# Down product of a quantised FFN: 128 stationary columns per token column in place of 121

## What is computed

```python
# layer 0: depthwise 25x25 convolution with a sparse mask (9x9 taps at a step of 3)
x = conv(x) * x + bias + x
# layer 1, on tokens t = (64, 3025, 96)
t = t + attn(layernorm(t))     # 96 -> 192, FFT over tokens, gate, inverse FFT, 192 -> 96
t = t + ffn(layernorm(t))
# ffn: every product takes operands rounded to fp8 (5 exponent, 2 mantissa bits), sums rounded to fp16
h = relu(qlinear(t, W1, b1))   # 96 -> 384
y = qlinear(h, W2, b2)         # 384 -> 96: the "down product"
```

## Time and profile before

| | |
|---|---|
| median of the runs shown | 5087.42 us |
| the profiled execution, first to last instruction (its time in the profile) | 5082.0 us |
| instructions | 121784 |
| TensorE matmuls busy | 4747.4 us, 93% |
| TensorE weight loads busy | 4227.9 us, 83% |
| VectorE busy | 3785.3 us, 74% |
| ScalarE busy | 3808.6 us, 75% |
| GpSimd busy | 2488.9 us, 49% |
| mean granted clock of TensorE | 0.964 |

### The profile page before, as it was taken

One profiled execution on the slowest core, in us unless ns is written; L12 is line 12 of the kernel. 1 busy time (PEld: TensorE's weight loads), 2 busy tenths in 40 slices (PEclk: granted clock), 3 DMA queues, 4 the chain that ended last, 5 costly groups with the idle time before them and its releaser, 6 DMA issues.

```text
span 5082.0 us, 121784 instructions
## 1 busy us (share of the span) xinstructions
PE 4747.4 (93%) x40842; PEld 4227.9 (83%) x40842; DVE 3785.3 (74%) x10870; ACT 3808.6 (75%) x7819; POOL 2488.9 (49%) x2603
## 2 busy tenths in 40 slices
PE   8999994699999999999999999999999999999974
PEld 7888884488888888888888888888888888888853
DVE  3444443247888888888888888888888888888884
ACT  3444442378888888888888888888888888888853
POOL 2335432144555555555555555555555555555542
PEclk9999997599999999999999999999999999999985
DMA  6777775256666666666666666666666666666541
GB/s 204 246 226 242 239 234 153 81 161 179 174 180 175 172 176 177 178 176 177 177 174 176 178 176 179 177 179 175 179 173 174 178 176 179 176 177 175 156 115 30
DMA packets 781423, 893.15 MB, mean 176 GB/s; under 512 B 236243, under 2 KB 689292, under 8 KB 768652
## 3 DMA queue, kind: packets, MB, share of 16 engines
q1 hardware_dynamic: 780556, 885.27, 63.5%
q10 hardware_dynamic: 264, 0.10, 0.0%
HBM read 500.64 MB, written 384.61 MB: 174 GB/s over the span
## 4 chain that ended last, share of the span: by engine, by line
PE 68%; DVE 8%; ACT 3%; issue 3%; DMA 0%; POOL 0%; DVEq 0%; POOLq 0%
PE ps L1021 12%; PE ps L1046 10%; PE ps L1033 10%; PE ps L1062 6%; PE ps L1061 6%; PE ps L1073 6%; PE ps L1085 5%; PE ps L1111 4%; PE ps L1122 4%; PE ps L1098 3%; PE ps L1133 1%; ACT ps L791 1%; DVE gv L946 1%; ACT spec L786 1%; DVE mean L896 1%
## 5 line engine op out<-in xcount | busy, mean ns | idle before, releaser
L721 POOL TENSOR_SCALAR gv<-gv 96x400 f32<-96x400 f32 (+1 forms) x512 | 599.6, 1171 | 1675.8 <-DVE xn L961 1587.6
L838 ACT ACTIVATE y<-ps 128x1089 f16<-128x1089 f32 (+1 forms) x512 | 572.9, 1119 | 328.7 <-PE ps L1111 328.7
L340 PE MATMUL cps<-toep,xin 114*128 114x190 f32 (+2 forms) x3456 | 775.9, 339 | 44.2 <-issue 25.5
L1046 PE MATMUL ps<-hid,fa 121*128 121x384 f32 (+1 forms) x2048 | 734.1, 441 | 82.9 <-DVE t L985 70.6
L1021 PE MATMUL ps<-fb,acol 100*96 100x100 f32 x7936 | 786.5, 252 | 15.0 <-DVE spec L953 14.5
L1021 PEld LDWEIGHTS ps<-fb,acol 100*96 100x96 f32 x7936 | 724.9, 164 | 25.3 <-issue 25.0
L286 ACT ACTIVATE xo<-cps 128x180 f32<-128x180 f32 (+3 forms) x576 | 367.4, 638 | 451.0 <-PE cps L343 451.0
L317 DVE SCALAR_TENSOR_TENSOR xo<-cps,xo 128x180 f32<-128x180 f32 (+3 forms) x576 | 362.7, 630 | 459.2 <-ACT xo L286 458.7
L1033 PE MATMUL ps<-w1t,xnt 97*121 97x192 f32 x3200 | 702.9, 330 | 0.7 <-ACT xnt L829 0.7
L1061 PE MATMUL ps<-w2t,spec 97*100 97x96 f32 x3968 | 673.2, 252 | 4.7 <-ACT y L838 4.7
L1062 PE MATMUL ps<-w2t,spec 96*100 96x96 f32 x3968 | 675.8, 252 | 0.0
(11 more groups left out here) (105 smaller groups left out, 10581.5 us busy)
## 6 DMA issues: line engine op xcount, KB each, us to landing
a_d<-arow SPq DMA_DIRECT2D x448, 288.0 KB, 3.9
acol<-a_d SPq DMA_DIRECT2D x192, 600.0 KB
xin<-in_items SPq DMA_DIRECT2D x96, 1008.0 KB
g_d<-mixed SPq DMA_DIRECT2D x256, 300.0 KB
tok<-x_d SPq DMA_DIRECT2D x64, 1134.4 KB
out<-o_sb SPq DMA_DIRECT2D x448, 136.1 KB
x_d<-xo SPq DMA_DIRECT2D x48, 990.0 KB, 11.9
grow<-g_d SPq DMA_DIRECT2D x128, 312.0 KB, 11.2
```

Of the source, the lines that this page charges most:

```text
L340: last = nc.tensor.matmul(ps[2 * (m % DEEP)][:, (r0 - o0) * GC:(r1 - o0) * GC], xb, toep[e % 2][0:GP, c, at * GC:(at + r1 - r0) * GC], sta ...
L721: nc.gpsimd.tensor_scalar(v, v, 0.0, None, ALU.max).then_inc(v_cut, 1)
L838: nc.scalar.activation(y16[n % 2][:, :, 0:w], ps[:, MIXP:MIXP + FM, 0:w], ACT.Copy).then_inc(y16_ready, 1)
L1046: nc.tensor.matmul(ps[0:M, ROW, 0:(s1 - s0) * H], fa[:, :], hid[part][:, 0:s1 - s0, :].rearrange("p j h -> p (j h)"), start=True, stop=Tru ...
```

## The change

The down product takes 128 columns of `hq` from j * 121 on: the 121 tokens of token column j and the 7 entries that follow. Its output covers 128 partitions of PSUM in place of 121; the last 7 aren't read. `hq` gets 8 more entries per row (492 in place of 484), so that the last piece stays inside of it, and is cleared once at the start.

```diff
-        hq = [sb(f"hq{s}", [128, FM, TOK], F8) for s in range(2)]
+        hq = [sb(f"hq{s}", [128, FM, TOK + 8], F8) for s in range(2)]
...
                 for v in y16:
+                    nc.vector.memset(v[:, :, :], 0.0)
+                for v in hq:
                     nc.vector.memset(v[:, :, :], 0.0)
...
                 for j in range(w):
                     for m in range(FM):
-                        last = nc.tensor.matmul(ps[0:U, DOWNP, C * j:C * (j + 1)],
-                                                hq[n % 2][:, m, j * U:(j + 1) * U], w2q[:, m, :],
+                        last = nc.tensor.matmul(ps[:, DOWNP, C * j:C * (j + 1)],
+                                                hq[n % 2][:, m, j * U:j * U + 128], w2q[:, m, :],
                                                 start=(m == 0), stop=(m == FM - 1))
```

## The result

The changed kernel takes 5047.06 us in the median of 4 runs (5035.8 to 5048.58), the kernel before 5087.9 (5086.44 to 5089.26): ratio 0.9919, 95% interval 0.9904 to 0.9935. It is 41 us faster.

What follows compares the result with a forecast made beforehand. TensorE was taken as the bound, with loads pacing its down matmuls. 45.1 + 0.8 + 6.4 - 0.7 = 51.6 us took the profiled 5082.0 to 5030.4; 5.4 carried over gave 5035.8, rounded up to 5037 (range 5028 to 5062).

Steps and rivals of the forecast that it cites:

- The load: Down product: fp8 loads of the full 128 columns are of a faster kind, near 100 ns instead of 137.
- Rival A: Down loads: no fast kind for hq, 128 columns are just 7 more; 17.6 us slower, 5105 us; chance 0.07.
- B: Down loads: only pieces starting at a multiple of 4 bytes load fast; 5.4 us gained, 5082 us; chance 0.06.
- Term 1, spacing: Down matmuls at full clock: 43 ns each; nine take 0.387 us, 0.103 less, and twelve 0.516, 0.144 less.
- rival C: Down matmuls: loads fast, but no load and matmul pair starts sooner than 52 ns; 15.8 us gained, 5072 us; chance 0.05.
- Term 1, images: Long stretch: 0.762 us saved per image, 45.1 us over 59.2 images, and 0.8 us more up to 4917.
- 66 are on it: Of 75 down matmuls per image, 66 lie on the chain; the 9 beside the detour through VectorE's statistics are off it.
- Piece follows piece on TensorE, except once: Chain of one image: it leaves TensorE only at 3011.10, through ScalarE and VectorE's layernorm statistics, and returns at 3019.16.
- Rival D: Long stretch: another engine takes over in part of the slots; with half keeping their length 28.7 us gained, 5059; chance 0.03.
- part 4: Longer hq rows, four-column cast in three runs: counted at nothing; 0.3 us once per image, 1 us at most in the drain.
- Term 2, drain: From 4917 us: nine down matmuls take 0.72 us, saving 0.25 per slot, 6.4 us in all, all on the chain.
- Term 3, setup: Before the second stage: VectorE clears two hq buffers, 0.34 us each, 0.7 us together, hidden by nothing.

Runs made afterwards that it cites:

- e3_127: Changed kernel with 127 stationary columns in the down product in place of 128: 5090.4 us, ratio 1.0012 to the kernel before.
- e8_ib_128: Changed kernel with 128 stationary columns in place of 100 in the fp32 inverse transform too: 5097.2 us in one run.
- e1_flat: Changed kernel with hq's rows kept at 484 and only the whole buffer 8 entries longer: median 5035.5 us, ratio 0.9898 to the kernel before.
- e11_y_rows: Changed kernel with the rows of y, the cast's source, 8 entries longer too: 5036.1 us in one run.
- e2_pad: Kernel before with only hq's longer rows and its memset, down product still at 121 columns: median 5081.8 us, ratio 1.0004 to the kernel before.
- e12_pool_pad: Changed kernel, rows of 492, with the first part of the layernorm statistics moved from VectorE to GpSimd: 4943.5 us in one run.
- e7_turn2_128: Changed kernel with 128 stationary fp8 columns in place of 96 in turn2 too: 5048.3 us in one run.

## Why the prediction was right, and where it was off

**The load** (its unknown). Right: 98 ns measured, "near 100" forecast. e3_127 shows that the number of columns is what does it, and e8_ib_128 that fp32 doesn't get it; no run here has a type between the two. Rival A is out for 128 columns and is nearly what 127 do. B is out by the 4800 records. This is what the Trainium skill says on the page "TensorE: Matmul & The Clock Gate", section "Weight-path perf modes — Fast Weight Load (FWL) and DoubleRow": 128 weights, not FP32. The runs agree, at 127 against 128 columns and at fp8 against fp32. The size that the prediction quoted from this section of the Trainium skill, a load shorter by 4x in theory and about 2x measured, they don't confirm: the records shrank from 137 to 98 ns, 1.4 times, and as the moving side now sets the pace, the spacing can't tell how short the load itself is.

**Term 1, spacing.** 43 ns forecast, 42 to 43 measured: the line from 121 and 484 moving columns down to 96 holds, and rival C is out.

**Term 1, images.** Forecast 0.762 us per image, measured 0.61. Two steps failed.
First, "66 are on it": 57 are. The nine beside the detour were rightly left out, but the nine of the next slot are off the chain too, since TensorE waits there again for the residual sum. The slot stayed at 7.65 us, before 7.64. The trace of the kernel before had this wait already (0.41 us at 3026.68 where 0.35 is normal, and rows part 1 0.15 us behind the residual sum in every image); I had read "Piece follows piece on TensorE, except once". That is 0.10 to 0.11 us. The other five groups of nine gave 0.11 each and the twelve 0.15, a little more than counted, so that e1_flat comes to 0.71. Rival D named this mechanism, with a chance of 0.03; it holds in one slot of eight beyond the detour's, not in half. My argument against it, ScalarE's 0.59 us of slack in one slot, looked at the wrong engine: VectorE, busy for 3088 of 3600 us, has slack on average and none around its statistics. ScalarE's wait in that slot didn't fall to the 0.49 us of the forecast either; it is still 0.59 on average.

Second, part 4, "counted at nothing": the longer rows of hq. I bounded the cast's growth by 0.3 us and it was 0.75, and I took its slot as one "where hq isn't urgent", which is true for hq and false for VectorE's queue. e1_flat and e11_y_rows show that a shorter cast brings back 0.10 and 0.07 us per image, e2_pad that the long one costs nothing while slots are longer, e12_pool_pad that it costs nothing without the burst.

The way from the cast to the detour can be read in the traces: VectorE's operations end late where a two-input operation (TENSOR_TENSOR) of GpSimd runs beside them. The bias operations of 364 elements that meet none take 304 to 306 ns on average, 315 at most, in the kernel before, the changed one and e1_flat (2000 to 4500 us). All that take more than 330 ns, 199 of 850 before and 327 of 861 in the changed kernel (246 in e1_flat), meet one, and 246 of those 327 end 0.10 us after it. So the long cast shifts the bias operations behind it onto GpSimd's work, above all those of the next slot (306 ns on average before, 523 now, 319 in e1_flat). It is the same with L898: in 41 of 41 images of the kernel before and in 40 of 41 of the changed one it ends 0.10 us after GpSimd's multiplication L747 (L749). It starts 0.09 us ahead of that operation before and 0.19 us ahead of it in the changed kernel, so its greater length is GpSimd's operation coming later. By which operations the delay gets from the slots behind the cast to this one stays open, and no run took GpSimd's operations away.

**Term 2, drain.** A slot at the lower clock gained 0.26 us, as forecast. But from eviction 464 to the end only 1.7 us were gained, where the terms give about 8. The step that failed is again part 4, "1 us at most" for the casts there. Six casts of four columns fall into that stretch, and nothing hides the later ones: the slot behind each of the last three is 7.27, 7.27 and 7.13 us, and 6.52, 6.52 and 6.38 in e1_flat, 0.75 us apart. With rows of 484 the whole stretch is 299.8 us, 5.4 below the changed kernel and 7.1 below before. The rest, some 1 to 2 us, can't be told from scatter: e7_turn2_128, which differs from the changed kernel in turn2 alone, needs 2.1 us more for the stretch.

**Term 3, setup.** 0.73 us for the memsets, right. The first up eviction comes 2.2 us later, but in the fourteen kernels, with nearly the same start, it lies anywhere from 1187.6 to 1201.4 us, so this says nothing.

**Sum.** For the profiled execution 5030.4 was forecast and 5046.8 measured: 8.6 us from 58 images, 6.4 from the drain, 1.5 from the start.

## What to carry to other kernels

If fp8 matmuls with few moving columns run at the pace of their loads, give them all 128 stationary columns, even if some are junk: 98 ns in place of 137 per load, 42 in place of 55 ns per matmul. It brings nothing where the moving side sets the pace (turn2) and costs 21 ns a matmul in fp32. When a group on the critical engine gets shorter, ask in which slots another engine has its burst, not how busy it is on average: here one burst of 3 us per image took a fifth of the gain (0.71 of 0.90 us were left; with the longer cast 0.61), and moving it to an engine that waited anyway brought the kernel from 5086 to 4922 us, together with the change and rows of 484. And padding a row changes the shape of every operation that writes it: keep the rows as they are, make the buffer as a whole a little longer, and let the last read run over.

## What I had not expected of the hardware

A VectorE cast of 128 x 1452 fp16 to fp8 takes 918 ns from one run to one run, 1168 from three runs of 484 to three, and 1666 from one run to three; the cast of 3 x 364 takes 918 as well. A 121 x 50 fp32 addition on VectorE took 843 to 941 ns on average when a two-input GpSimd operation ran beside it, and ended 0.10 us after that one; an addition of the same shape, from other buffers and with none beside it, took 212 ns (L901 before). A bias operation of 128 x 364 fp16 took 306 ns alone and up to 973 beside such operations.
